# Taking a subtraction of the linear steps from VectorE to GpSimd, in two late slots of each step

## What is computed

```
h = layernorm(x) * (1 + ca) + sa
q, k, v = split(h @ Wqkv.T + bqkv)
q = (elu(q) + 1 + 1e-4) / sqrt(8);  k = elu(k) + 1 + 1e-4
num = q @ cumsum(k v^T);  den = q . cumsum(k) + 1e-4
x = x + ga * layernorm((num / den) @ Wout.T + bout)
```

## Time and profile before

| | |
|---|---|
| median of three runs | 714.31 us (713.6 to 716.53) |
| the profiled execution | 713.35 us |
| its span, first to last instruction | 711.2 us |
| busy: PE, DVE, ACT, POOL | 635.7, 613.3, 494.0, 413.6 us |
| linear attention (slots of steps 0 to 7) | from about 36 to 237 us of the span |

### The profile page before, as it was taken

One profiled execution on the slowest core, in us unless ns is written; L12 is line 12 of the kernel. 1 busy time (PEld: TensorE's weight loads), 2 busy tenths in 40 slices (PEclk: granted clock), 3 DMA queues, 4 the chain that ended last, 5 costly groups with the idle time before them and its releaser, 6 DMA issues.

```text
span 711.2 us, 16640 instructions
## 1 busy us (share of the span) xinstructions
PE 635.7 (89%) x5448; PEld 329.8 (46%) x5448; DVE 613.3 (86%) x1568; ACT 494.0 (69%) x1007; POOL 413.6 (58%) x929
## 2 busy tenths in 40 slices
PE   4498789889888789899999999999999999799994
PEld 2276566666555412122333333333323323498994
DVE  6868999998978898889999999999999994676552
ACT  3534555766654438788888888888888889755662
POOL 4122465575574565144766787887777771566553
PEclk9789999999999959999999999999999999999998
DMA  6663142351352412116430120302103000465600
GB/s 180 150 243 128 53 135 76 105 178 63 118 179 90 134 45 91 45 45 180 149 90 1 40 86 13 113 24 77 48 21 105 25 12 35 121 183 173 175 31 12
DMA packets 42341, 67.05 MB, mean 94 GB/s; under 512 B 7965, under 2 KB 35584, under 8 KB 39057
## 3 DMA queue, kind: packets, MB, share of 16 engines
q1 hardware_dynamic: 38480, 56.73, 25.9%
q0 software_dynamic: 3296, 8.41, 3.3%
q10 hardware_dynamic: 480, 0.85, 0.5%
HBM read 43.22 MB, written 23.04 MB: 93 GB/s over the span
## 4 chain that ended last, share of the span: by engine, by line
PE 46%; DVE 24%; ACT 12%; POOL 8%; issue 7%; SPq 1%; DMA 0%; ACTq 0%; POOLq 0%; DVEq 0%
DVE arena L1545 11%; PE bank L1056 8%; ACT arena L1974 6%; PE pair L1307 5%; PE pair L1045 5%; PE bank L1017 4%; DVE arena L1378 3%; PE bank L1316 2%; PE pair L1316 2%; POOL arena L695 2%; DVE arena L1407 2%; PE bank L902 2%; ACT arena L1943 2%; PE bank L913 2%; PE bank L887 2%
## 5 line engine op out<-in xcount | busy, mean ns | idle before, releaser
L1974 ACT ACTIVATE arena<-pair 128x512 f32<-128x512 f32 x506 | 278.1, 603 | 50.4 <-PE pair L1045 48.4
L1545 DVE TENSOR_REDUCE arena<-bank 128x1 f32<-128x512 f32 x388 | 251.3, 682 | 7.1 <-PE bank L1017 6.1
L1045 PE MATMUL pair<-q_stack,k_stack 64*128 64x512 bf16 x506 | 158.0, 386 | 5.8 <-ACT arena L1974 5.1
L1017 PE MATMUL bank<-k_stack,q_stack 63*128 63x512 bf16 x388 | 137.4, 396 | 8.8 <-DVE arena L1545 5.0
L1056 PE MATMUL bank<-arena,values 128*9 128x512 f32 x1024 | 134.4, 597 | 1.6 <-ACT arena L1974 1.5
L1378 DVE TENSOR_TENSOR arena<-bank,cst 128x512 f32<-128x512 f32 x128 | 82.2, 683 | 15.6 <-PE bank L887 14.9
L1545 DVE TENSOR_REDUCE arena<-pair 128x1 f32<-128x512 f32 x124 | 84.2, 679 | 1.5 <-PE pair L1017 1.1
L1017 PEld LDWEIGHTS bank<-k_stack,q_stack 63*128 63x128 bf16 x388 | 33.3, 93 | 109.3 <-DVE arena L1545 24.9
L695 POOL TENSOR_TENSOR arena<-arena 128x32 f32<-128x32 f32 (+6 forms) x312 | 68.4, 219 | 24.4
L1045 PEld LDWEIGHTS pair<-q_stack,k_stack 64*128 64x128 bf16 x506 | 40.6, 93 | 48.3 <-ACT arena L1974 26.2
L1890 ACT ACTIVATE arena<-bank,den_eps 128x512 f32<-128x512 f32 x32 | 21.7, 678 | 43.1 <-PE bank L913 43.1
(11 more groups left out here) (299 smaller groups left out, 1261.7 us busy)
## 6 DMA issues: line engine op xcount, KB each, us to landing
linear_parts<-arena SPq DMA_DIRECT2D x8, 768.0 KB, 3.7
q_stack<-linear_parts SPq DMA_DIRECT2D x48, 128.0 KB, 2.9
softmax_parts<-arena SPq DMA_DIRECT2D x8, 768.0 KB, 4.1
q_stack<-softmax_parts SPq DMA_DIRECT2D x48, 128.0 KB, 2.9
k_stack<-softmax_parts SPq DMA_DIRECT2D x48, 128.0 KB, 2.9
k_stack<-linear_parts SPq DMA_DIRECT2D x42, 128.0 KB, 2.9
arena<-in_L_ffn_w_dram SPq DMA_DIRECT2D x16, 256.0 KB, 4.5
v_all<-token_rows SPq DMA_DIRECT2D x20, 192.5 KB, 2.7
```

The source lines that it names most:

```text
L1017: pe.matmul(bank[:], qs[b % 2][rows, slot, qt * P:(qt + 1) * P], ks[b % 2][rows, slot, :], start=True, stop=True).then_inc(d_s_m, 1)
L1045: pe.matmul(score_bank(s)[:], ks[u][rows, 2 * g + x, kt * P:(kt + 1) * P], qs[u][rows, 2 * g + x, :], start=True, stop=True).then_inc(d_s_ ...
L1545: dve.reduce_max(mx[:, m % 2, col:col + 1], bank[:], AX).then_inc(d_s_mr, 1)
L1974: act.activation(pt[:, kt % 2, x, half, :], score_bank(s)[:], ACT.Exp, scale=SCALE).then_inc(d_s_e, 1)
```

## The change

`a_rest` gets a copy on POOL, which is used in steps 0 to 5, so for batches 2 to 7: q in slot 6, k in slot 7, behind all that POOL does in slots 0 to 5. DVE keeps `a_rest` in steps -2 and -1, for batches 0 and 1. Twelve instructions move, each 128 x 512 float32. POOL's copy waits for the first part like DVE's, and for the last part of the same buffer.

```diff
+                def a_rest(a, z):
+                    pool.wait_ge(a_s_p1, 2 * a + z + 1)
+                    wait(pool, a_s_p3, 2 * a + z - 1)
+                    pool.tensor_tensor(a_r1[:, z, :], feature(a, z), a_parts[:, 3 * z, :], ALU.subtract).then_inc(a_s_r1, 1)
+
...
                         if d == 5 and has(s - 1):
                             x_ready(s - 1)
+                        if d == 6 and has(s + 2) and s >= 0:
+                            a_rest(s + 2, 0)
+                        if d == 7 and has(s + 2) and s >= 0:
+                            a_rest(s + 2, 1)
...
                         if d == 6 and has(s + 2):
                             a_feature(s + 2, 1)
-                            a_rest(s + 2, 0)
-                        if d == 7 and has(s + 2):
+                            if s < 0:
+                                a_rest(s + 2, 0)
+                        if d == 7 and has(s + 2) and s < 0:
                             a_rest(s + 2, 1)
```

## The result

The changed kernel took 718.06 us (median of 7 runs, 715.93 to 718.83) against 714.7 us before (7 runs, 713.6 to 716.53) on the same chip. The ratio is 1.0042, 95% interval 1.0028 to 1.0057. The forecast was 713.8 us with a range of 711.5 to 717.0.

What follows compares the result with a forecast made beforehand. No engine alone was taken to bound the kernel; the chain changes hands. +0.6 (step 0), 0 (steps 1 to 4) and -1.1 (step 5) gave -0.5 us; 712.85 plus 0.96 for the median made 713.8 us, range 711.5 to 717.0.

Steps and rivals of the forecast that it cites:

- the prices: Twelve subtractions on POOL, taken at 1.16 us each, with bounds of 0.68 and 1.65 us.
- part 2: Who waits for POOL in steps 1 to 4: ACT's `a_second_part` of q 0.57 us late, zero on the chain.
- part 3, step 0: POOL's first subtraction blocks DVE's `a_feature` of k, and ACT carries the delay into the chain: +0.6 us.
- steps 2 to 4: Slots 6 and 7 and the slot after: ACT's delay is taken up by idle time, so zero.
- case for steps 2 to 4 at 2.4 GHz: If PE stays at the high clock there, ACT's `c_first_part` is what is late, 0.29 before L1538: 712.9 us.
- part 4, step 5: Slot 7 and after: `masked` is early, PE's products lose 0.40 us of idle, next `masked` earlier: -1.1 us.
- first uncertainty: PE's clock: if step 5 falls to 1.2 GHz, its gain goes and 0.40 us more is lost: +1.0, 715.3 us.
- part 2, step 1: `numerators_out` late by 0.57 us, PE's products at about 86.95, DVE's `masked` at 87.41 anyway: zero.
- which work the clock's low stretches fall on: Anywhere in the kernel: DVE's earlier `masked` changing this would make the forecast wrong; no size given.
- C: Rival: DVE's 12.6 us become idle time, POOL follows `a_feature` in step 0, PE's clock binds step 5: 714.3 us, chance 0.15.
- A: Rival: DVE is on the chain wherever busy, all 12.6 us come back: 701.7 us, chance 0.03; its half 709.4, 0.04.
- B: Rival: ACT's order passes the delay on in each step, 3.5 us slower: 717.8 us, or 720.7; chance 0.11.

Runs made afterwards that it cites:

- fourth trace of the changed kernel: The changed kernel run again unaltered on another chip, against the kernel before: 716.2 us, ratio 1.0042.
- ACT's order changed: The changed kernel with ACT's `a_second_part` of q moved to the end of slot 7, in step 1 alone, against the kernel before: 715.28 us, 0.9994.
- before, once more: The kernel before, run again with no change on a chip where it takes 715.37 us: 714.56 us, ratio 0.9994.
- the first experiment: Four kernels, each moving the subtractions of some steps only, against before: step 0 1.0003, step 1 1.0010, steps 2 to 4 1.0007, step 5 0.9993.
- the changed kernel's second: The changed kernel run again unaltered on a slower chip, against the kernel before at 728.26 us: 729.06 us, ratio 1.0015.
- feature first: The changed kernel with POOL's first subtraction of step 0 waiting for DVE's `a_feature` of k, against the kernel before: 730.73 us, ratio 1.0028.
- Both edits: Subtractions on POOL and ACT's `a_second_part` of q at the end of slot 7, both from step 1 on, against before: 711.87 us, 0.9948.
- the new order alone: The kernel before with ACT's `a_second_part` of q at the end of slot 7, all subtractions still on DVE: 731.11 us, ratio 1.0032.
- its fourth: The kernel before, run again with no change on another chip: 712.97 us, ratio 0.9995.
- the order changed in all steps: The changed kernel with ACT's `a_second_part` of q at the end of slot 7 in steps 0 to 5, against before: 724.86 us, 0.9948.

## Why the prediction was wrong

**Right: the prices.** POOL's groups, changed kernel, answer to the earlier trace rows:

```profile
L630 POOL TENSOR_TENSOR arena<-arena 128x512 f32<-128x512 f32 x6 | 6.9, 1155 | 1.3 <-ACT arena L1936 1.3
L630 POOL TENSOR_TENSOR arena<-fq_all,arena 128x512 f32<-128x512 f32 x6 | 6.9, 1154 | 9.8 <-ACT arena L1936 9.8
```

1.16 us was taken. ACT's wait before `a_second_part` is 1.61 to 1.63 us instead of 1.05, the 0.57 of part 2.

**Right: part 3, step 0.** +0.6 forecast, +0.56 or +0.57 in all three traces of the changed kernel tabled and 0 wherever step 0 stayed on DVE. The mechanism is the one described, down to DVE's end 0.54 us after POOL's.

**Right: steps 2 to 4 give nothing.** Step 3 into 4, changed kernel, answers to the earlier trace rows:

```profile
139.35 1.29 DVE L1387 TENSOR_TENSOR arena<-bank,cst 128x512 f32<-128x512 f32 x2 [1.43 <-PE bank L896]
140.56 0.68 DVE L1547 TENSOR_TENSOR arena<-pair,arena 128x512 f32<-128x512 f32 x1
...
137.12 0.63 ACT L1940 ACTIVATE arena<-arena 128x512 bf16<-128x512 f32 x1 [1.61 <-POOL arena L630]
...
139.67 0.58 ACT L1968 ACTIVATE arena<-pair 128x512 bf16<-128x512 f32 x1
140.15 0.67 ACT L1900 ACTIVATE arena<-bank,den_eps 128x512 f32<-128x512 f32 x1
```

The freed time stands before `masked`, 1.43 us where 0.34 was; `c_rest` still starts as soon as `masked` is through, and ACT's `c_first_part` ends before it. At the low clock the step is the same as before's; at the full clock a step of before gains 0.43 on its own low-clock self and a step of the changed kernel 0.25. So here the edit costs 0.2 us a step at the full clock and nothing at the low one. The prediction's case for steps 2 to 4 at 2.4 GHz, 0.29 us gained in each, is close to these 0.25, but they are the clock's gain and not the edit's. (Its "-0.9 in all" comes on top of the -0.5, so -1.4 in all; the 712.9 beside it is reckoned so.)

**Right, and it hangs on the clock: part 4, step 5.** In the fourth trace of the changed kernel step 5 ran at 2.4 GHz and shifted -1.08, for -1.1 forecast. Timeline of that trace, answers to the earlier trace rows:

```profile
190.97 0.69 DVE L1387 TENSOR_TENSOR arena<-bank,cst 128x512 f32<-128x512 f32 x1 [1.07 <-PE bank L896]
...
189.99 0.61 PE L911 MATMUL bank<-fq_all,arena 128*128 128x128 f32 x4
190.53 0.40 PE L896 MATMUL bank<-q_stack,k_stack 63*128 63x128 bf16 x8
```

The 0.40 us of idle before `products` is gone. But in the five other tabled traces with step 5 moved the low clock lay there, and step 5 shifted 0.42 to 0.44. The forecast had that as its first uncertainty, with 0.4 lost; it was the commoner case, and not the one in the sum.

**Wrong: part 2, step 1.** It said "DVE's `masked` is at 87.41 anyway: zero too". It came out at +1.10, +1.10, +1.05 and +1.07 in the four tabled traces with the step moved and the old order, 0 in those of before, and -1.92 with ACT's order changed. Up to `masked` the reading was right. Counted without the 0.80 us by which the step began late, PE's products start at 86.90 (86.95 was forecast) and `masked` at 87.34, against 87.41 before, though now it waits for PE and no longer for its own list. The step that failed is the wait behind that: the account stopped at `masked`, took PE to wait for ACT longer by the 0.57 us of delay alone, and put what such a wait does to PE's clock at nothing.

What the runs show in its place is one long wait of PE and a slow return. Before, DVE's late `masked` held PE back, so that PE's idle time with PE at 2.4 GHz was in two pieces, 1.26 us for DVE and 0.79 for ACT (before, once more). In the first trace of before PE was at 1.2 GHz until 84.1, so the first piece was filled and the second was 0.60. The change takes DVE's delay away. PE then runs ahead and has all its idle time before `turn`: 1.26 + 0.79 and ACT's new 0.57 are 2.62, and 2.70 was measured. Then it is at 1.2 GHz from 88.8 to 92.3. Its next products come 2.26 us after the last ones (87.70 to 89.96), where they come 1.79 us after them at 2.4 GHz with ACT's order changed (86.41 to 88.20). An estimate from these rows: with 1.79 they would start at 89.49, without the 0.80 at 88.69, and before they are at 88.75. So with PE at 2.4 GHz throughout the zero would have held, and the 1.1 us are the price of the slow return. With PE at 1.2 GHz up to 85.4, as in the pair of the first experiment, PE comes late to the wait, stands 0.60 us, no stretch at 1.2 GHz follows, and the edit costs nothing.

That ACT's standing is the cause is shown: the one instruction's place removes the wait, the low stretch and the loss. That PE's long wait is what brings the low clock is the reading that fits. Five traces have the wait of 2.70 us (the four tabled and the changed kernel's second), and in all five PE falls to 1.2 GHz 0.4 to 1.7 us after its return; in the other thirteen no such stretch starts between 86 and 90 us. One of them, feature first, has the old order and steps 1 to 5 moved, but there PE was at 1.2 GHz from 80.5 to 87.3, stood 0.60 us, and step 1 shifted 0.81. PE's other long wait, 2.02 us at 216 to 226 us, is followed by a low stretch within 2 us in 14 of the 16 traces that have it, and the two traces without it have none there. But other stretches at 1.2 GHz have no wait over 2 us ahead of them, and idle time and clock were not varied one without the other.

**Wrong: no term for untouched work.** The sum ended at step 5, and the text named "which work the clock's low stretches fall on" only as something that would upset it. The changed kernel lost 2.6 us behind step 5. Windows at its two largest places, changed kernel:

```profile
249.30:273.20 23.90, 21.64 (x56) 5.03 (x57) 22.14 (x53) 9.38 (x21) 11.83 (x24) 0.50 0.11 38
...
617.90:621.30 3.40, 2.84 (x14) 2.87 (x15) 1.10 (x5) 3.37 (x8) 2.69 (x7) 0.50 0.62 145
```

and before, its stretch at 1.2 GHz, and the work that the changed kernel does at 617.9:

```profile
247.90:268.50 20.60, 18.52 (x51) 4.25 (x51) 20.23 (x50) 8.18 (x18) 11.09 (x23) 0.50 0.12 39
614.30:617.70 3.40, 2.59 (x20) 2.19 (x20) 1.97 (x10) 3.37 (x8) 2.68 (x7) 1.00 0.54 132
```

At the first place the low clock lasted 23.9 us instead of 20.5 and the stretch grew by 0.9 us; at the second it was there instead of not, and the work took 1.06 us longer. In the table the rest is 2.1 to 3.8 in the six traces with the subtractions of steps 1 to 5 on POOL, and 0 to 2.0 in the four traces of before (the first of them is the zero). The groups just don't overlap and their means lie 2.3 us apart. It is there with ACT's order changed too (3.1 in step 1 alone, 2.8 from step 1 on), though these two kernels aren't slower than before. But the first trace of before, from which all is counted, is one of its fast ones (713.35 us, against a median of 714.7), either kernel varies by about 2 us with itself, before has the stretch near 614 in two of its four traces too, and nothing in the instructions ties this part to the change. That a kernel shifted by 1 to 2 us meets other low stretches behind is argued, not shown. It stays open how much of the loss is due to it. The part that is shown, steps 0 and 1, is 1.7 us of a measured 2.7 (3.4 in the first comparison).

**The rivals.** C (nothing moves) had steps 2 to 4 right, step 5 right in five of six tabled traces (bound by PE's clock), and step 0 wrong. A is out: DVE's 11 us came back nowhere with the old order. B named the nearest time, 717.8 us, by a mechanism that is not the one, so by luck: a delay passed on in each step. Steps 2 to 4 pass none on at the low clock and 0.2 at the high one. Its core, that ACT's order is what turns POOL's slower subtraction into a loss, is right for step 1. And the new order shows what the frozen one hid. Both edits, step 3, which ran at the full clock there, all engines:

```profile
134.24 1.29 DVE L1387 TENSOR_TENSOR arena<-bank,cst 128x512 f32<-128x512 f32 x2 [1.07 <-PE bank L896]
...
131.81 1.63 ACT L1918 ACTIVATE arena<-x_all,arena 128x128 f32<-128x128 f32 x4
133.34 0.57 ACT L1944 ACTIVATE h_all<-pair 128x512 f32<-128x512 f32 x1
133.82 0.58 ACT L1968 ACTIVATE arena<-pair 128x512 bf16<-128x512 f32 x1
134.30 0.62 ACT L1940 ACTIVATE arena<-arena 128x512 bf16<-128x512 f32 x1
...
132.34 1.16 POOL L630 TENSOR_TENSOR arena<-fq_all,arena 128x512 f32<-128x512 f32 x1
133.46 1.16 POOL L630 TENSOR_TENSOR arena<-arena 128x512 f32<-128x512 f32 x1
```

ACT runs without a gap while POOL subtracts from 132.34 to 133.50, and takes the result at 134.30. That step shifted -1.5 us; steps 2 and 4, partly at the low clock, shifted nothing. So the idle time of DVE can be had in part, once the engine behind POOL does not stand for it, and only where PE's clock is high.

## What to carry to other kernels

When work goes from a full engine to a slower free one, the engine that reads the result next is where to look: if it is strictly in order and the read stands early in its list, it stands for the slower producer, and everything behind the read is late. Move the read behind what is ready; here the move alone was 0.15 to 0.55% slower, the new order alone 0.3% slower, and both together 0.5% faster than before, with the step in which POOL blocked DVE or without it.

Having taken work from an engine, ask who stood for it. Their idle time doesn't go, it moves to their next wait. Here two waits of PE, 1.26 and 0.79 us, and a delay of 0.57 became one wait of 2.70, and a forecast of zero became 1.1 us, because PE came back from it at 1.2 GHz. So work out each wait of PE anew, once at each of its two clock levels, and give the return from a long one a price.

## What was not expected of the hardware

PE's stretches at 1.2 GHz lie in other steps in other executions of one and the same kernel: they begin at 80.7, 104.6, 131.9 and 159.2 us in the first trace of before, and at 131.8 alone between 40 and 220 in its fourth. With the order changed in all steps, one trace had none between 40 and 217 us, and its linear steps were 7 us shorter. A single trace of this kernel is good to about 2 us, which is as large as the effect that was looked for.
